# Second spectral mixer: transforms over sums and differences of the two token tiles, 256 spectrum numbers for 288, projection and inverse one turn later

## The reference

```python
pooled = x.mean(axis=(1, 2))
h = jnp.square(relu(pooled @ fc1_w)) * mlp_scale + mlp_bias
routeing = softmax((h @ fc2_w).reshape(B, 4, 192), axis=1)
xp = act1_scale * jnp.square(relu(x @ pwconv1_w)) + act1_bias      # 96 -> 192 channels
xf = rfft2(xp, axes=(1, 2), norm='ortho')                         # 16 x 9 complex numbers a channel
weight = einsum('bfc,hwf->bhwc', routeing, bicubic(complex_weights))
xo = irfft2(xf * weight, s=(16, 16), norm='ortho')
out = xo @ pwconv2_w                                              # 192 -> 96 channels
```

## Time and profile before

| | |
|---|---|
| time, three runs | 1013.63, 1014.53 and 1016.04 us, median 1014.53 |
| profiled execution | 1016.98 us, of which the span from the first to the last instruction is 1015.2 us |
| busy share of the span | PE 86%, PEld 70%, DVE 63%, POOL 55%, ACT 44% |
| TensorE's granted clock, mean over the span | 0.924 of full speed |
| the second mixer | from about 728.5 us (its constants) to about 867 us, about 138 us |

### The profile page before, as it was taken

How to read it: one execution, slowest core, us unless ns; L and a number is a source line. 1 busy time by engine, 2 the same in 40 slices (tenths; PEclk the granted TensorE clock), 3 DMA queues, 4 the chain that set the end, 5 groups by cost and what they waited for, 6 DMA issues and landing times.

```text
span 1015.2 us, 24331 instructions
## 1 busy us (share of the span) xinstructions
PE 869.9 (86%) x8876; PEld 712.8 (70%) x8876; DVE 640.1 (63%) x1770; ACT 445.6 (44%) x875; POOL 559.7 (55%) x871
## 2 busy tenths in 40 slices
PE   4677667768889999969998799999679998999997
PEld 4555555656767888857887678888658777688886
DVE  6765778547775756557778347777535664367755
ACT  1433364145645444427676254444133442544441
POOL 5342452243427786856654266878425545576865
PEclk9877779579999999979999799999869998999999
DMA  8500010000022101000001001100000001001120
GB/s 182 89 4 0 14 27 1 1 1 1 1 55 57 48 24 47 2 2 1 0 1 40 24 25 38 35 23 25 2 1 1 1 0 47 26 25 31 40 72 18
DMA packets 39050, 26.16 MB, mean 26 GB/s; under 512 B 27288, under 2 KB 31753, under 8 KB 38913
## 3 DMA queue, kind: packets, MB, share of 16 engines
q1 hardware_dynamic: 37964, 24.20, 9.6%
q10 hardware_dynamic: 998, 0.80, 0.3%
HBM read 8.08 MB, written 1.57 MB: 10 GB/s over the span
## 4 chain that ended last, share of the span: by engine, by line
PE 56%; DVE 13%; issue 12%; POOL 9%; ACT 8%; ACTq 1%; DMA 1%; POOLq 0%; DVEq 0%
PE PS L1462 16%; PE PS L1437 7%; PE PS L1438 6%; PE PS L1441 4%; PE PS L1380 3%; PE PS L1549 2%; PE PS L1540 2%; PE PS L1530 2%; ACT H L575 2%; POOL H L488 2%; ACT H L656 2%; PE PS L1252 2%; PE PS L1299 1%; POOL rs L434 1%; DVE H L1153 1%
## 5 line engine op out<-in xcount | busy, mean ns | idle before, releaser
L617 ACT ACTIVATE H<-PS,B 128x512 f32<-128x512 f32 x288 | 176.9, 685 | 214.6 <-PE PS L1441 214.0
L1462 PE MATMUL PS<-M,H 128*64 128x96 f32 x4608 | 203.6, 249 | 8.1 <-DVE X L1086 8.1
L1462 PEld LDWEIGHTS PS<-M,H 128*64 128x64 f32 x4608 | 194.7, 139 | 19.0 <-DVE X L1086 8.6
L420 POOL TENSOR_TENSOR msum<-stats 128x4 f32<-128x4 f32 (+1 forms) x61 | 14.2, 233 | 316.6 <-DVE stats L762 279.7
L1086 DVE SCALAR_TENSOR_TENSOR X<-PS,G,X 128x96 f32<-128x96 f32 (+1 forms) x384 | 121.0, 317 | 74.0 <-PE PS L1462 63.2
L1438 PE MATMUL PS<-FHL,M1l 128*128 128x512 f32 x192 | 76.2, 397 | 0.0
L1437 PE MATMUL PS<-XH,M1h 128*128 128x512 f32 x192 | 76.2, 397 | 0.0
L1518 PE MATMUL PS<-FDFT,H 128*128 128x288 f32 (+1 forms) x256 | 70.9, 434 | 4.2 <-DVE H L1126 4.0
L464 POOL TENSOR_TENSOR ex<-euler,dl 128x16 f32<-128x16 f32 x24 | 69.8, 2910 | 7.8 <-DVE dl L1050 7.6
L456 POOL TENSOR_TENSOR PF<-G,B 128x1536 f32<-128x1536 f32 x24 | 66.1, 2756 | 10.0 <-DVE G L1077 10.0
L434 POOL TENSOR_TENSOR rs<-ve,half 128x4 f32<-128x4 f32 (+1 forms) x61 | 66.3, 1086 | 4.8
(11 more groups left out here) (239 smaller groups left out, 1986.7 us busy)
## 6 DMA issues: line engine op xcount, KB each, us to landing
FHL<-XH SPq DMA_DIRECT2D x36, 192.0 KB, 2.5
FHL<-XL SPq DMA_DIRECT2D x36, 64.0 KB, 2.2
X<-XH SPq DMA_DIRECT2D x12, 192.0 KB, 2.5
raw<-L_ffn_w SPq DMA_DIRECT2D x3, 576.0 KB, 4.7
M<-L_ffn_w SPq DMA_DIRECT2D x3, 576.0 KB, 6.0
X<-x SPq DMA_DIRECT2D x4, 384.0 KB, 6.9
XH<-XL SPq DMA_DIRECT2D x24, 64.0 KB, 1.9
out<-X SPq DMA_DIRECT2D x8, 192.0 KB, 2.4
```

The source lines that it names most:

```text
L617: act.activation(H[p][:, c, :], bank(UB[c]), ACT.Gelu, bias=B1[e][:, c:c + 1]).then_inc(gelu_a, 1)
L1462: ins = pe.matmul(Y[rows, x * C:(x + 1) * C], H[p][:, j, t * P + rows.start:t * P + rows.stop], M2[e][:, j, :], start=c == 0, stop=c == CH ...
```

## The change

The image's two token tiles are its upper and lower eight rows. A wave over the rows is the same in both tiles for even row frequencies and has its sign turned for odd ones. The changed kernel makes the sum and the difference of the two tiles (`HA`) and transforms the sum to the even and the difference to the odd frequencies, each with a matrix of 128 columns (`FD3`). The mirrored numbers in the first and the ninth column of the half spectrum are left out, so that an image and channel has 256 numbers and not 288. Spectrum, weights (four pieces of 128, one matrix product of 512 columns), products, sums, projection (two pieces of 128) and inverse (two pieces, `GD3`, for each token tile) are laid out after that. Scale and bias go from DVE to ACT (an Identity activation). The projection and inverse of group g are done in turn g+1, and the routing's exponential, product, transposes and low part likewise a turn later; the walk has one more turn (8). The transform of a turn is done in two halves, one image each, with `route_in` between them. The experts' first use of a bank no longer waits for x; their first `down` does.

```diff
+        FD3 = sg2[:, 0:4 * HF].rearrange("p (e n) -> p e n", e=2)
+        GD3 = sg[:].rearrange("p (k n) -> p k n", k=3)
...
-        XF = [hflat[0][0:C, o:o + 1152].rearrange("p (c r i f) -> p c r i f", c=2, r=2, i=2) for o in (2048, 3200)]
+        XF = [hflat[0][0:C, o:o + 1024].rearrange("p (c r i f) -> p c r i f", c=2, r=2, i=2) for o in (2048, 3200)]
+        HA = hflat[0][:, 4352:4352 + GT * MED].rearrange("p (t m) -> p t m", t=GT)
+        OF = hflat[1][:, 2304:2304 + 1024].rearrange("p (c i n) -> p c i n", c=2, i=2)
+        PF3 = hflat[1][:, 3456:3456 + 384].rearrange("p (i n) -> p i n", i=2)
...
-        DB, PB, IB = ((0, 4, 6, 5), (6, 5, 4, 0)), ((5, 1), (2, 1)), (3, 3)
+        DB, PB, IB = ((0, 4, 6, 5), (6, 0, 4, 2)), ((5, 1), (6, 4)), (3, 5)
...
+                sp.wait_ge(wt_v, 7)
+                sp.dma_start(FD3, a["k_dft3"]).then_inc(wfft, 16)
+                sp.dma_start(GD3, a["k_idft3"]).then_inc(wfft, 16)
...
-                        pool.wait_ge(prod_v, 3 * (4 * g + n) + 3)
+                        pool.wait_ge(prod_v, 2 * (4 * g + n) + 2)
                         pool.wait_ge(pp_pe, 16 + 2 * g)
-                        pool.tensor_tensor(OU[0:C, j // 2, j % 2, :], MA[:, j, :, :].rearrange("p r n -> p (r n)"),
-                                           MB[:, j, :, :].rearrange("p r n -> p (r n)"), ALU.add).then_inc(y_p, 1)
+                        o = OF[0:C, j // 2, j % 2, :].rearrange("p (e r n) -> p e r n", e=2, r=2)
+                        for r in range(2):
+                            ins = pool.tensor_tensor(o[:, :, r, :], MA[:, j, r, :].rearrange("p (e n) -> p e n", e=2),
+                                                     MB[:, j, 1 - r, :].rearrange("p (e n) -> p e n", e=2), ALU.add)
...
+                        act.wait_ge(sq_a, 4 * g + 4 + 2 * i + 1)
+                        after(act, h_v, 2 * s)
+                        act.activation(HH[kc][:, ts, :], R[kc][:, ts, :], ACT.Identity, bias=SBc[kc][:, 1:2],
+                                       scale=SBc[kc][:, 0:1]).then_inc(sq_a, 1)
...
+                        act.activation(PF3[:, i, :], bank(PB[kc][i], 2 * C), ACT.Copy).then_inc(ps_a, 1)
...
             def mixer3(g, p):
+                if has(g, 1, 2):
+                    routing_exp(g + 1)
                 if has(g, 1):
                     mix_relu(1, 5, g)
+                if has(g, 1, 2):
+                    routing_hi(g + 1, 1 - p)
+                if has(g, -1):
+                    mix_out(1, g - 1)
                 if has(g, 2, 2, PREPS[6]):
                     prep_hi(40 + g + 2, p)
                 if has(g, 1):
-                    mix_spectrum(1, g, p)
+                    mix_spectrum(1, g, p, (0, 1))
                 if has(g, 2, 2):
                     routing_relu(g + 2)
-                if has(g, 0):
-                    mix_out(1, g)
-                if has(g, 2, 2):
-                    routing_exp(g + 2)
-                    routing_hi(g + 2, p)
-            mixer_walk(act, mixer3)
+                if has(g, 1):
+                    mix_spectrum(1, g, p, (2, 3))
+            mixer_walk(act, mixer3, GROUPS)
             moe(7, 6, 2)
 
 
...
+                    if kc == 1:
+                        dve.wait_ge(sq_a, 4 * g + 4 + 2 * i + 2)
+                        dve.tensor_tensor(HA[:, 2 * i, :], HH[1][:, 2 * i, :], HH[1][:, 2 * i + 1, :], ALU.add)
+                        dve.tensor_tensor(HA[:, 2 * i + 1, :], HH[1][:, 2 * i, :], HH[1][:, 2 * i + 1, :], ALU.subtract)\
+                           .then_inc(h_v, 1)
...
+                def products(order):
+                    for n in order:
+                        j = BY_IMAGE[n]
+                        c, i = j // 2, j % 2
+                        W = bank(j, 8 * HF, C).rearrange("p (k r f) -> p k r f", k=2, r=2)
+                        dve.wait_ge(w_pe, 4 * g + n + 1)
+                        dve.wait_ge(xf_a, 32 + 4 * g + n + 1)
+                        after(dve, y_p, 4 * g)
+                        dve.tensor_tensor(MA[:, j, :, :], XF[p][:, c, :, i, :], W[:, 0], ALU.mult).then_inc(prod_v, 1)
+                        dve.tensor_tensor(MB[:, j, :, :], XF[p][:, c, :, i, :], W[:, 1], ALU.mult).then_inc(prod_v, 1)
+                if has(g, 1, 2):
...
+                    routing_norm(g + 1)
                 if has(g, 1):
                     mix_h(1, g)
                 if has(g, 0):
...
+                    products((0, 1))
+                if has(g, 1, 2):
+                    routing_out(g + 1, 1 - p)
+                if has(g, 0):
+                    products((2, 3))
+                if has(g, -1):
+                    mix_x(1, g - 1, xu[6])
+                if prep:
+                    prep_lo(m + 2, p, g + 2 if has(g, 2, 2) else None)
                 if has(g, 3, 2, PREPS[6]):
                     prep_stats(m + 3, g + 3, xu[5], xu[6])
                 if has(g, 2, 2):
                     routing(g + 2)
-                if has(g, 0):
-                    mix_x(1, g, xu[6])
-                if has(g, 2, 2):
-                    routing_out(g + 2, p)
-            zero_rows(1, [OU, PSs])
-            mixer_walk(dve, mixer3)
+            zero_rows(1, [OF])
+            mixer_walk(dve, mixer3, GROUPS)
             moe(7, 6, 2)
 
 
...
+                        if isinstance(g, int) and g == 0:
+                            pe.wait_ge(xu[phase - 1], GROUPS)
...
+            def mix_dft(kc, g, images=BY_IMAGE):
                 s = 8 * kc + g + 1
-                for j in BY_IMAGE:
+                for j in images:
                     c, i = j // 2, j % 2
                     pe.wait_ge(h_v, 2 * s + i + 1)
                     if kc == 0 and DB[0][j] in B2B[0:2]:
                         after(pe, z_a, 4 * g + 1 + B2B.index(DB[0][j]))
-                    if kc == 1 and j == 3:
-                        after(pe, prod_v, 12 * g + 3)
+                    if kc == 1 and j in BY_IMAGE[2:]:
+                        after(pe, prod_v, 8 * g + 2 * BY_IMAGE.index(j) - 2)
+                    if kc == 1:
+                        spectrum = bank(DB[1][j], 4 * HF, C).rearrange("p (r e n) -> p e r n", r=2, e=2)
+                        for half_ky in range(2):
+                            ins = pe.matmul(spectrum[:, half_ky], HA[:, 2 * i + half_ky, c * C:(c + 1) * C], FD3[:, half_ky, :],
+                                            start=True, stop=True)
+                        ins.then_inc(dft_pe, 1)
+                        continue
                     for kk in range(2):
...
+                    for n in range(3 - kc):
                         for c in range(2):
-                            ins = pe.matmul(PS[0:C, PB[kc][i], n * C:(n + 1) * C], OU[:, c, i, n * C:(n + 1) * C],
-                                            PO[kc][:, c, :], start=c == 0, stop=c == 1)
+                            if kc == 0:
+                                o, w = PS[0:C, PB[0][i], n * C:(n + 1) * C], OU[:, c, i, n * C:(n + 1) * C]
+                            else:
+                                o, w = PS[:, PB[1][i], n * C:(n + 1) * C], OF[:, c, i, n * P:(n + 1) * P]
+                            ins = pe.matmul(o, w, PO[kc][:, c, :], start=c == 0, stop=c == 1)
...
+                            w, x = GD3[:, n * (1 + kk), :], PF3[:, :, n * C:(n + 1) * C]
+                        ins = pe.matmul(o, w, x, start=n == 0, stop=n == 2 - kc)
...
-                if has(g, 0):
-                    pe.wait_ge(xf_a, 32 + 4 * g + 4)
                 if has(g, 1):
+                    if has(g, 0):
+                        pe.wait_ge(xf_a, 32 + 4 * g + 2)
+                    if isinstance(g, int):
+                        after(pe, xu[6], g - 1)
                     mix_h(1, 5, g, p)
                 if has(g, 0):
                     pe.wait_ge(rt_x, g + 1)
                     pe.wait_ge(xf_a, 32 + 4 * g + 4)
+                    after(pe, prod_v, 8 * g)
                     for j in BY_IMAGE:
-                        if j == 2:
-                            after(pe, ps_a, 16 + 2 * g)
-                        if j == 3:
-                            after(pe, xu[6], g)
-                        pe.matmul(bank(j, 3 * FR, C), RT[p][:, j, :], CWS[:], start=True, stop=True).then_inc(w_pe, 1)
+                        pe.matmul(bank(j, 8 * HF, C), RT[p][:, j, :], CWS[:], start=True, stop=True).then_inc(w_pe, 1)
+                if has(g, 1, 2):
+                    route_turn(g + 1)
+                if has(g, -1):
+                    if has(g, 1):
+                        pe.wait_ge(r_a, 2 * (8 + g + 1) + 1)
+                    mix_channels(1, g - 1)
+                    if has(g, 1):
+                        pe.wait_ge(r_a, 2 * (8 + g + 1) + 2)
+                    else:
+                        pe.wait_ge(xu[6], g - 1)
+                    mix_tokens(1, g - 1)
                 if has(g, 2, 2, PREPS[6]):
                     prep_turn(40 + g + 2, False, (rt_x, g + 2 if has(g, 2, 2, 8) else GROUPS))
                 if has(g, 1):
```

(83 more changed lines are left out.)

49 lines of the change are left out of this document (18 added, 31 removed).

## The result

The changed kernel took a median of 1006.52 us (1005.43 to 1007.63, 4 runs), the kernel before 1015.25 us on the same chip (1013.63 to 1016.04, 4 runs): a ratio of 0.9907 with a 95% interval of 0.9889 to 0.9924. It is faster by 0.9%, and 0.9 us from the forecast of 1005.6. A later comparison of the same two gave 0.9921 (0.9895 to 0.9947).

The account below looks back on a forecast made before the run. PE's issue time was taken to bound a steady turn. Full-clock savings of 22.0 us, less 13.1 for clock falls and DVE collisions, gave -8.9 from the median 1014.53: 1005.6 us; own range 1001 to 1010, with rivals 995 to 1016.

Parts of the forecast that it names:

- the two forecast places: PE waits in a steady turn: 1.2 us before the inverse for ACT, 1.3 before route_in for DVE's pooled sum.
- the forecast 3.15: PE's work in a steady turn was to fall by 3.15 us, from 12.86 to 9.71.
- Turns -1 and 0: Mixer's first two turns: 18.8 us at full clock for 25.80 before, a saving of 7.0.
- The walk: Step-by-step timing of the engines' in-order queues through the mixer's turns at full clock; a steady turn came to 12.35 us.
- The full-clock turn: Steady mixer turn without a clock fall: 12.35 us for 14.08 before, carried by ACT and DVE.
- A fall: Drop of PE's clock to half level: one allowed in each of turns 0 to 5, at 1.2 us, +7.2 altogether.
- Collisions on DVE: DVE instructions with two SBUF inputs, like the new sum and difference, collide with POOL's work: +1.3 us.
- The end: Mixer turns 6 to 8: 20.5 us at full clock for 24.00 before, plus 2.6 for projection and inverse at half clock.
- That the clock holds: Rival 1: no clock falls in the mixer, only 1.3 us of DVE collisions come off the 22.0: 993.8 us; 15%.
- That the clock stays down: Rival 2: PE stays at half clock in turns 0 to 5: about 1034 us, or 1022 for two thirds; 16%.
- That the chain is longer by a us a turn: Rival 3: two more handovers, slower Identity or pair, 5 x 1.2 = 6 us: about 1012 us; 13%.
- That everything is given back: Rival 4: waits and falls equal PE's saving, 14 us a turn: 1013 to 1016 us; 6%.

Follow-up runs that it names:

- experiment 4: Changed kernel with the forward transform of the first of a turn's two images computed twice on PE, output unchanged: 1006.16 us, ratio 0.9925 to the kernel before.
- experiment 3: Changed kernel with scale and shift moved from ACT's Identity back to DVE, as a tensor_scalar ahead of its pair: 1005.14 us, ratio 0.9921 to the kernel before.
- Experiment 7: Changed kernel with DVE's pooled sum ahead of XL's low part, and route_in in another bank: 1003.15 us, ratio 0.987 to the kernel before.
- experiment 2: Changed kernel's order and bodies with the old 288-number transforms, scale and bias on DVE (the move alone): 1012.34 us, ratio 0.9971 to the kernel before.
- experiment 1: Changed kernel's new sizes in the old order, with the banks and the x wait of before: 1036.88 us, ratio 1.0231 to the kernel before.
- Experiment 6: The new sizes in the old order, with the whole forward transform computed twice, output unchanged: 1030.52 us, ratio 1.0143 to the kernel before.

## Why the prediction held, and where its terms were off

**The mechanism was right.** PE idles at the two forecast places, released by the forecast engines: 1.36 and 1.29 for 1.2 and 1.3. PE's busy time in a full-clock turn is 10.23; in the window of turn 4 before it was 13.19, so it fell by 2.96 for the forecast 3.15. More work for PE is free (experiment 4), and shortening either chain shortens the full-clock turn (experiments 3 and 7). The forward transform was forecast at 1.85; its 16 products are now in two runs of 1.04 and 1.11 with their drains, 1.9 without them. Inverse 1.37: the row's 1.54 less its drain. The projection, 1.95 with its drain for a forecast of 1.8, is right as well.

**Turns -1 and 0** came out at 21.95. The walk gave 18.8, with 2.0 for a turn 0 that begins before the clock has risen and 1.2 for a fall: 22.0. Both happened, and the fall ran on into turn 1. The start was 7.56 for 7.5, and turn 0 14.39 for 11.3 + 3.2.

**Turns 1 to 5** came out at 67.07, against 61.8 + 6.0 of falls + 1.3 of collisions = 69.1. Three terms were off, and they cancelled in part:
- *The full-clock turn* was 12.35, and is 12.88. The Identity was sized as one of the pair relu and square, 0.47; it has a step of 0.62 (809.31 less 808.69), and the square that feeds it 0.55. Two halves took 3.37 (807.61 to 810.98) for the walk's 3.05. Experiment 3, which takes it from ACT, comes to 12.13. The walk's turn was 0.5 too low, 2.6 in five.
- *A fall* was priced at 1.2 and costs 0.4 to 0.5: 13.3 against 12.88. The fall covers the weights, the routing transposes and the projection (in turn 2 the last of the expansion too), which lie beside ACT's chain; the wait before the inverse drops from 1.36 to 0.42. Turns 2 to 4 paid that, turn 1 with its lower clock of 0.81 paid 1.4, turn 5 nothing: 2.7 in five for 6.0.
- *Collisions on DVE*, 1.3: not there. The pair took 0.36 and 0.35 and the routing's product 0.18, where it took 0.60 before. In the trace of before, POOL's wide multiply of `XN` lies under that product; in the new turn it starts at 808.34, after the product and before the pair. The GPSIMD Engine Reference of the Trainium skill (Specifications) names the shared way to SBUF; the rows agree that it matters which POOL work is beside the DVE instruction, and no run here moved the pair into it. The rows also show the form of the collision. In the kernel before the product starts 0.27 after the multiply, takes 0.60 and ends 0.03 to 0.04 after it, in each of turns 0 to 5. In experiment 2 it starts 0.5 to 0.6 after the multiply, takes 0.25 to 0.34 and again ends 0.03 to 0.04 after it, in all five turns where they overlap. So the product is held until the multiply ends, and not slowed by a fixed amount, so that 0.4 for each instruction of the pair was the wrong form of the price. DVE's products of a spectrum, which read one operand from PSUM, take 0.41 to 0.42 under POOL's sums as well as beside no POOL work.

**The end** came out at 23.06 at a clock of 0.86; the walk gave 20.5, and 2.6 for half clock: 23.1. Experiment 7 ended at a clock of 1.00 in 21.03, so at full clock the walk was 0.5 too low and the clock cost 2.0 for 2.6.

**The sum.** The profiled executions differ by 11.1 us for the 8.9 forecast. Turns 1 to 5 make 2.0 of the difference. The start's 0.4 cannot be read: the mixer begins at 743.81 for 743.60, but at 742.02 in the changed kernel's other execution. The medians differ by 8.7. That this is within 0.2 us of the forecast is partly luck: in the loop alone, a turn 2.6 too short in five stood against 3.3 too much for falls and 1.3 for collisions that did not come.

**The rivals.** That the clock holds is refuted: it fell in turns 0, 2, 3 and 4 and at the end of turn 5. The fall of turn 0 came at the end of a wait of 2.96 us for the pooled sum. TensorE: Matmul & The Clock Gate of the Trainium skill (Why this matters for your kernels) warns of longer idle gaps than those of turns 1 to 5, whose two are at most 1.4 us; the measurement decides, and here the clock fell behind turns that had only two such gaps and a train of 2-column products, though not behind turn 4, which had them too. That the clock stays down did not happen to this kernel, but experiment 1 came near it, with mean clocks of 0.68 to 0.78 and turns of 17.2 to 18.6: the clock rose in each turn, and fell again. The rival was a real one; the move is what kept this kernel from it. That the chain is longer by a us a turn is half true (0.5), and was paid for by the cheaper falls. That everything is given back is refuted by both comparisons.

**What the prediction did not see** is how far the two halves of the change depend on each other. It priced the sizes and the move in one walk, which was enough for the total. My expectation for the sizes alone was wrong by more than 20 us. Experiment 6 shows that the clock has a share in it and leaves at most some 1.6 us a turn to the chain; an exact division stays open, since the two were not parted by a run at full clock.

## What to carry to other kernels

When the bound engine gets lighter, walk the in-order queues of the others at once: only 1.2 of the 3.0 us that PE was relieved of in a full-clock turn reached the time, and the rest became waiting. A smaller computation with a longer chain of handovers may need a reordering to pay: here it lost 2.3% alone, the reordering alone gained 0.3%, and both together 0.9%. Price a clock fall by its length and by what lies beside it. One of 3.4 us cost 0.4 to 0.5 us a turn where ACT's longer chain hid it, and 1.2 in experiment 3, where that chain was shorter; falls of some 6.8 us (turns at 0.77) cost 2.1 and 2.8 (experiments 7 and 3).
